# Tokenizer in products of two tokens with overlapped groups, and score products of 32 rows in two attention stages

## The reference, cut to what matters

```python
def _forward(signal):                       # (64, 4000)
    interp = cubic_interpolate_1d(signal, 0.25)
    windows = interp[:, idx]                # (64, 249, 64)
    kw = 0.5 * (windows + 1.3) ** 2 + 0.5 * exp(-0.5 * (windows - 0.7) ** 2)
    M = abs(fft(kw, axis=-1))
    Mmax = max(M, axis=-1, keepdims=True)
    Mt = M * sigmoid(M - 0.12 * Mmax)
    return soft_minimum(Mt, 0.9 * Mmax)     # -log(exp(-a) + exp(-b))
...
q, k, v = heads(x @ Wq.T + bq), heads(x @ Wk.T + bk), heads(x @ Wv.T + bv)   # 4 heads of 16
attn = softmax(einsum('bhnd,bhmd->bhnm', q, k) * 16 ** -0.5)
```

## Time and profile before

| what | us |
|---|---|
| median of 3 runs (lowest, highest) | 5498.31 (5491.29, 5501.21) |
| the profiled execution, its own time | 5488.11 |
| its span, first to last instruction | 5486.3 |
| TensorE busy | 4628.9 (84%) |
| VectorE busy | 2953.6 (54%) |
| ScalarE busy | 2398.0 (44%) |
| mean granted clock of TensorE | 0.858 |

### The profile page before, as it was taken

How to read it: one execution, slowest core, us unless ns; L and a number is a source line. 1 busy time by engine, 2 the same in 40 slices (tenths; PEclk the granted TensorE clock), 3 DMA queues, 4 the chain that set the end, 5 groups by cost and what they waited for, 6 DMA issues and landing times. The chain is left out here.

```text
span 5486.3 us, 115823 instructions
## 1 busy us (share of the span) xinstructions
PE 4628.9 (84%) x33352; PEld 3139.7 (57%) x33352; DVE 2953.6 (54%) x8221; ACT 2398.0 (44%) x6049; POOL 2090.7 (38%) x2436
## 2 busy tenths in 40 slices
PE   4509999566779999889997657699999999979999
PEld 4405666334656666556665644366666666646665
DVE  1144555255535565444443446577777777735554
ACT  3323343242112333334442223277777777735555
POOL 0002222275623343222224756354444444433333
PEclk9998777667957797799996556699999999989999
DMA  0010010132210010043331112100000000033332
GB/s 9 8 34 21 20 22 19 27 99 66 56 26 21 23 27 23 23 93 82 74 79 37 42 42 53 41 8 12 9 12 9 12 9 12 8 67 73 72 73 62
DMA packets 483609, 206.37 MB, mean 38 GB/s; under 512 B 451744, under 2 KB 474454, under 8 KB 483286
## 3 DMA queue, kind: packets, MB, share of 16 engines
q1 hardware_dynamic: 483414, 204.24, 16.5%
HBM read 158.26 MB, written 45.91 MB: 37 GB/s over the span
## 5 line engine op out<-in xcount | busy, mean ns | idle before, releaser
L3346 POOL TENSOR_TENSOR att_P<-att_P,att_rden 125x498 f32<-125x498 f32 x512 | 520.3, 1016 | 640.0 <-DVE att_rden L3617 640.0
L3533 ACT ACTIVATE att_P<-att_pS,att_nb 125x249 f32<-125x249 f32 x1024 | 472.8, 476 | 17.0 <-DVE att_nb L3625 17.0
L2638 DVE TENSOR_TENSOR moe_hT<-moe_silu,moe_pH 128x498 f32<-128x498 f32 x384 | 258.9, 674 | 324.8 <-ACT moe_silu L2624 324.8
L3954 ACT ACTIVATE sw_hT<-sw_pH,sw_b 128x498 f32<-128x498 f32 x512 | 318.3, 673 | 243.4 <-PE sw_pH L3908 243.4
L3449 PEld LDWEIGHTS att_pP<-att_ident,att_P 124*125 124x125 f32 (+1 forms) x2048 | 262.1, 187 | 187.5 <-issue 187.5
L3449 PE MATMUL att_pP<-att_ident,att_P 124*125 124x124 f32 (+1 forms) x2048 | 351.6, 294 | 9.8 <-POOL att_P L3346 8.4
L2624 ACT ACTIVATE moe_silu<-moe_pH 128x498 f32<-128x498 f32 x384 | 225.3, 587 | 284.5 <-PE moe_pH L2581 198.7
L3625 DVE TENSOR_REDUCE att_nb<-att_pS 125x2 f32<-125x498 f32 x512 | 322.6, 667 | 47.1 <-PE att_pS L3437 45.4
L3540 ACT ACTIVATE att_PTr<-att_pP 125x498 f32<-125x498 f32 x512 | 304.7, 595 | 91.6 <-PE att_pP L3449 85.7
L578 POOL TENSOR_TENSOR att_norm_centered<-att_F,att_norm_sum 125x256 f32<-125x256 f32 (+1 forms) x128 | 85.1, 665 | 645.8 <-DVE att_norm_sum L573 645.5
L1013 PE MATMUL att_pS<-att_kT,att_qT 16*125 16x249 f32 x1024 | 302.3, 478 | 2.1 <-ACT att_kT L1119 1.3
(11 more groups left out here) (460 smaller groups left out, 11403.4 us busy)
## 6 DMA issues: line engine op xcount, KB each, us to landing
moe_share<-mixing SPq DMA_DIRECT2D x64, 498.0 KB
sw_share<-mixing SPq DMA_DIRECT2D x64, 498.0 KB
ffn_W<-in_ffn_pairs SPq DMA_DIRECT2D x64, 192.0 KB
att_F<-h_stream SPq DMA_DIRECT2D x192, 62.5 KB
att_X<-h_stream SPq DMA_DIRECT2D x192, 62.5 KB
h_stream<-att_H SPq DMA_DIRECT2D x64, 62.5 KB
ffn_F<-h_stream SPq DMA_DIRECT2D x64, 62.5 KB
ret_F<-h_stream SPq DMA_DIRECT2D x64, 62.5 KB
```

The source lines that it names most:

```text
L3346: g.tensor_tensor(own, own, bc(rden[:, j % 2, c, :], T), ALU.mult).then_inc(*scaled.one())
L3533: ins = a.activation(P[:, r, c, t, :], pS[:, 2 * r + c, t * T:(t + 1) * T], ACT.Exp, bias=nb[:, r, c, t:t + 1], accum_out=den[:, r, c, t:t ...
L3954: a.activation(hT[:, k % 4, :, :], pH[:, place, :, 0:T], ACT.Relu, bias=b1[:, k:k + 1]).then_inc(*hid_ready.one())
```

## The change

The tokenizer is written anew. The host lays the samples out turned (`x_turned`: samples by signals), so nothing is transposed on the chip. Two neighbouring tokens share a product: 36 samples (20 plus a step of 16) are the rows, 128 columns of taps give both tokens' 64 points. 25 groups of `PG` = 5 such products (ten tokens) are written out without a loop. SP loads four groups ahead (`AHEAD`). Each engine's order is by slots: in slot s TensorE interpolates group s and makes the spectrum of group s-1, and the other engines follow the same order, with two buffers of everything. The spectrum is made in halves: each token's 64 points lie in one half of the partitions and give 64 rows of the output there. The passes behind the loop are cut into three chunks of groups (0 to 11, 11 to 22, 22 to 25); a chunk's steps are put into the slots 1 to 6 after its last group, and its store on SP into slot 9 or behind the loop. The sigmoid is one activation.

In attention 0 and attention 1 the score products read 32 rows (`ROOM`) in place of 16 and 17; positions, columns and order are the same.

```diff
-    WG = 8
-    GROUPS = T // WG
-    TAPS = 20
+    PG = 5
+    Q = (T + 1) // 2
+    GROUPS = Q // PG
+    TAPS = 36
     NF = 33
+    COLS = PG * BATCH
+    CHUNKS = ((0, 11), (11, 22), (22, GROUPS))
+    AHEAD = 4
...
+        def chunk_at(s, step):
+            return [c for c, (lo, hi) in enumerate(CHUNKS) if hi + step == s]
...
             def _(sp):
...
+                def load(s):
+                    if s >= AHEAD:
+                        sp.wait_ge(*interpolated.after(s - AHEAD))
+                    k = s % AHEAD
+                    src = A["x_turned"][s * 32 * PG:s * 32 * PG + TAPS, :]
+                    sp.dma_start(xs[:, k, :, :], bass.AP(src.tensor, src.offset, [[BATCH, TAPS], [32 * BATCH, PG],
+                                                                                 [1, BATCH]])).then_inc(
+                        *loaded[k].one())
+                    sp.dma_start(wt[:, k, :, :], A["const_taps"][:, s * PG:(s + 1) * PG, :]).then_inc(
+                        *loaded[k].one())
...
+                load(0)
...
+                for s in range(1, GROUPS):
+                    load(s)
+                    for c in chunk_at(s, 9):
+                        store(c)
+                for c in range(len(CHUNKS)):
+                    if CHUNKS[c][1] + 9 >= GROUPS:
+                        store(c)
...
             def _(pe):
...
+                for s in range(GROUPS + 1):
+                    if s < GROUPS:
+                        u, k = s % 2, s % AHEAD
+                        pe.wait_ge(*loaded[k].after(s // AHEAD))
+                        pe.wait_ge(*squared.after(s - 2))
+                        for q in range(PG):
+                            ins = pe.matmul(pI[:, u, q * BATCH:(q + 1) * BATCH], wt[:, k, q, :], xs[:, k, q, :],
+                                            start=True, stop=True)
+                        ins.then_inc(*interpolated.one())
...
+                        g, u = s - 1, (s - 1) % 2
+                        pe.wait_ge(*windows_ready.after(g))
+                        pe.wait_ge(*squares_ready.after(g - 2))
+                        for q in range(PG):
+                            for w2 in range(2):
+                                r = slice(w2 * 64, (w2 + 1) * 64)
+                                ins = pe.matmul(pM[r, u, q * 2 * NF:(q + 1) * 2 * NF],
+                                                kw[r, u, q * BATCH:(q + 1) * BATCH], dft[r, :], start=True, stop=True)
+                        ins.then_inc(*spectrum.one())
...
             def _(a):
...
+                    for c in chunk_at(s, 1):
+                        q = pairs(c)
+                        a.wait_ge(*power_ready.after(CHUNKS[c][1] - 1))
+                        a.activation(mag[:, q, :], mag[:, q, :], ACT.Sqrt).then_inc(*magnitude_ready.one())
+                    for c in chunk_at(s, 3):
+                        q = pairs(c)
+                        a.wait_ge(*excess_ready.after(c))
+                        a.activation(d[:, q, :], d[:, q, :], ACT.Sigmoid).then_inc(*masked.one())
+                    for c in chunk_at(s, 5):
...
@@ attention 0, by query and by key @@
-                        ins = pe.matmul(pS[:, 2 + s % 2, t * T:t * T + T], qT[r:r + D, u, b, t * OFF:t * OFF + PT],
-                                        kT[r:r + D, u, b, :], start=True, stop=True, tile_position=(r, 0))
+                        ins = pe.matmul(pS[:, 2 + s % 2, t * T:t * T + T], qT[r:r + ROOM, u, b, t * OFF:t * OFF + PT],
+                                        kT[r:r + ROOM, u, b, :], start=True, stop=True, tile_position=(r, 0))
...
-                        ins = pe.matmul(pS[:, s % 2, t * T:t * T + T], kT[r:r + DV, u, b, t * OFF:t * OFF + PT],
-                                        qmT[r:r + DV, b, :], start=True, stop=True, tile_position=(r, 0))
+                        ins = pe.matmul(pS[:, s % 2, t * T:t * T + T], kT[r:r + ROOM, u, b, t * OFF:t * OFF + PT],
+                                        qmT[r:r + ROOM, b, :], start=True, stop=True, tile_position=(r, 0))
@@ attention 1, by query and by key @@
-                    return pe.matmul(pS[:, 2 + s % 2, out], qT[r:r + D, u % 2, b, q], kT[r:r + D, u, b, k],
+                    return pe.matmul(pS[:, 2 + s % 2, out], qT[r:r + ROOM, u % 2, b, q], kT[r:r + ROOM, u, b, k],
...
-                    return pe.matmul(pS[:, s % 2, out], kT[r:r + DV, u, b, k], qmT[r:r + DV, b, q],
+                    return pe.matmul(pS[:, s % 2, out], kT[r:r + ROOM, u, b, k], qmT[r:r + ROOM, b, q],
```

More of the change, by code:

```diff
@@ L387, in stage_tokenizer @@
[L387 to L403, removed]
+        names = "interpolated squared kernels_done windows_ready spectrum squares_ready power_ready"
@@ new lines, in store @@
+                def store(c):
+                    q = pairs(c)
+                    sp.wait_ge(*out_ready.after(c))
+                    for w2 in range(2):
+                        n = min(q.stop, Q - w2) - q.start
+                        dst = h[:, 2 * q.start + w2:2 * q.start + w2 + 1, :]
+                        sp.dma_start(bass.AP(dst.tensor, dst.offset, [[T * C, BATCH], [2 * C, n], [1, C]]),
+                                     out[w2 * BATCH:(w2 + 1) * BATCH, q.start:q.start + n, :]).then_inc(
+                            *stored[c].one())
@@ new lines, in _ @@
+                load(0)
+                for half in range(2):
+                    sp.dma_start(dft[half * 64:(half + 1) * 64, :], A["const_dft"][:, :]).then_inc(*const_loaded.one())
+                for s in range(1, GROUPS):
[5 more added lines that the diff above has]
+                        store(c)
+                for c in range(len(CHUNKS)):
+                    sp.wait_ge(*stored[c].after(0))
@@ L428, in _ @@
             @block.tensor
             def _(pe):
[L430 to L453, removed]
@@ L458, in _ @@
                 a.wait_ge(*memset_done.after(0))
[L460 to L481, removed]
@@ L512, in _ @@
-                groups(v, body)
-                v.wait_ge(*magnitude_ready.after(0))
-                link(v.reduce_max(top[:, :], mag[:, :, :], AX.X))
-                v.tensor_scalar(thr[:, 0, :], top[:, :], 0.12, None, ALU.mult)
-                link(v.tensor_scalar(thr[:, 1, :], top[:, :], 0.9, None, ALU.mult))
-                v.tensor_tensor(d[:, :, :], mag[:, :, :], bc(thr[:, 0, :], NF), ALU.subtract).then_inc(
-                    *excess_ready.one())
-                v.wait_ge(*excess_exp.after(0))
@@ L520, in _ @@
-                link(v.tensor_scalar(d[:, :, :], d[:, :, :], 1.0, None, ALU.add))
-                link(v.reciprocal(d[:, :, :], d[:, :, :]))
-                link(v.tensor_tensor(mag[:, :, :], mag[:, :, :], d[:, :, :], ALU.mult))
-                v.tensor_tensor(lg[:, :, :], mag[:, :, :], bc(thr[:, 1, :], NF), ALU.subtract).then_inc(
-                    *gap_ready.one())
-                link(v.tensor_tensor(mag[:, :, :], mag[:, :, :], bc(thr[:, 1, :], NF), ALU.min))
-                v.wait_ge(*gap_log.after(0))
@@ L4111, in interpolation_taps @@
         w[p // 64, idx - (16 * (p // 64) - 2), p % 64] += val
-    return w
+    both = np.zeros((36, (T + 1) // 2, 2, 64), f)
+    for k in range(2):
+        n = (T + 1 - k) // 2
+        both[16 * k:16 * k + 20, 0:n, k, :] = w[k::2].transpose(1, 0, 2)
+    return both.reshape(36, (T + 1) // 2, 128)
 def constants():
```

179 lines of the change are left out of this document (105 added, 74 removed).

## The result

The changed kernel takes 5081.4 us (median of 4 runs, 5079.0 to 5084.7), the kernel before beside it 5494.8 (5467.1 to 5501.2): a ratio of 0.926, with a 95% interval from 0.922 to 0.929. The profiled execution took 5083.5 us against 5488.1, so 404.6 us went.

What follows compares the result with a forecast made beforehand. The tokenizer was taken as a chain across engines, attention 0 and 1 as bound by TensorE at a falling clock. Gains 241 + 110 + 60 = 411 us bring 5488.1 to 5077, forecast 5087 as median, range 5030 to 5190.

Steps and rivals of the forecast that it cites:

- Tokenizer: gain 241: Tokenizer rewritten with overlapping groups and chunked tail: from 404.5 to 163 us, gain 241, with both ends 225 to 262.
- the bounds' low end of 3.7: TensorE's time for one tokenizer group of ten tokens: 3.7 to 4.8 us, taken as 4.2.
- the case with its halves side by side: Tokenizer's twenty spectrum records a group: 1.3 us if both array halves work side by side, 2.4 one after the other.
- 8 + 3: Tokenizer loop: 8 us for chunk 0's ScalarE activations beyond free time, 3 us for loads waiting behind its store.
- nearly throughout: Sign of being right: TensorE in the tokenizer busy nearly throughout, at about 4.2 us a group.
- 18 by share and 25: Tokenizer's last two stores: 18 us as 56% of the old one, 25 if half was fixed cost; 22 taken.
- Attention 0: 110 forecast: Score products of 32 rows keep attention 0's clock up, pairs about 14.1 us: gain 110 us, between 75 and 120.
- Attention 1: 60 forecast: Wider score products in attention 1, a low stretch staying in most pairs: gain 60 us, between 30 and 95.
- The 20 us for the first pairs: Attention 1's first two or three pairs, low before, could give 20 us more at the upper clock.
- Rival (1): Rows don't count for the clock, only a busy engine; both attentions stay, only the tokenizer gains: 5257 us, chance 0.12.
- Rival (2): The lower clock level keeps itself up in attention 1, which then gives nothing: 5147 us, chance 0.15.
- Rival (3): A wider score product costs time in both attentions; the kernel ends slower, between 5760 and 6260 us, chance 0.02.

Runs made afterwards that it cites:

- the products put into the two thin places: Changed kernel plus seven mask products a pair in attention 1, four ahead of the value products, three ahead of the turn of the heads' output: 5032.7 us.
- the four with fill and increments: Changed kernel with added mask products and VectorE increments: all edits 5017.5 us; increments split 5010.7; split, two chunks 5050.5; two chunks, 105 increments in tokenizer loop 5003.8.
- the increments: Changed kernel with 190 semaphore increments added to VectorE's program behind the tokenizer's last copy: 5057.5 us.

## Why the prediction was right

5087 us were forecast for the median, 5081.4 came, in the range. The sum was 411 us, the profiled execution lost 404.6. That is closer than its terms were, and so in part luck: against the forecast the tokenizer gave 8 us more, attention 0 gave 20 more, attention 1 gave 13 less, and attention 3 and the untouched stages beside it took 16 and 5, which were not in the sum. The 10 us that the forecast adds for the median didn't come either (profiled 5083.5, median 5081.4).

- **Tokenizer: gain 241, measured 249.** Up to the last group, 123 forecast and 121.3 measured, by errors that cancel. A group takes 3.62 us, below the bounds' low end of 3.7: the ten interpolation records took 2.39 as costed from the old spectrum, so the products kept the lower level's price, as counted, and the spectrum cost what the case with its halves side by side gave, 20 records in 1.36 (1.3 forecast). I took 4.2, midway; 25 groups are 15 us less. The chunks in the loop cost 22.7 (with one chunk the last power sum ends at 98.6) where I had 8 + 3. TensorE's waits split it: 10.0 while chunk 0 passes through the loop (five waits for VectorE's sum between 59 and 83 us), near the 8 from ScalarE's free 2.1 us a slot; 7.0 for the loads behind chunk 0's store, where I had 3 and at most 6; and some 5 at the loop's end, where chunk 1's first steps stand on ScalarE and VectorE ahead of the last group's. That last part I had at nothing: the step that failed is the one that counted chunk 0 alone, and beside it the price of the loads. The tail was 34.4 against 40: 16.8 to chunk 1's output (18), and 17.6 for the stores, where I took 22 between 18 by share and 25. That the share fits is luck, since the whole store became shorter too: with one chunk it takes 26.1 us (145.73 to 171.80) where it took 32.8, for the same bytes, and no run shows why. TensorE was busy all through a group, but 91 of 153 us of the stage: "nearly throughout" was wrong.
- **Table loads.** One is 1.28 us, and the activation starts 0.02 us after its end (122.82 + 1.28, 124.12). The drain that the Trainium skill (ScalarE: Activation LUTs, What ACT_TABLE_LOAD costs) puts on top isn't there, and the tail isn't 10 us longer.
- **Attention 0: 110 forecast, 130 measured, above its own range.** The mechanism was right (though the stretch that I gave for the clock's fall, 560 to 566, lies behind it: the score products have the lower level's 0.62 us from 551.81 on). The size of a pair was not: 13.68 us and not 14.1, since what a pair loses at the lower level isn't in proportion to the time it spends there (3.0 us for 6.3 in the pair of 16.70, 7.8 for 18.1 in that of 21.50). And none of TensorE's waits came back: it was busy 382.4 of 383.0 us.
- **Attention 1: 60 forecast, 47 measured.** The low stretch stayed in most pairs, as said, and the products put into the two thin places took it away. Pairs went from 21.63 to 20.45 us. The 20 us for the first pairs didn't come: they stayed at 30.5 and 27.5, the clock rising only 126 us into the stage, as before.
- **Attention 3: not in the sum, 16 us lost.** I followed every engine's program inside the touched stages and nothing of it outside. This is the one mechanism that I missed.

Rival (1) falls by the runs with 18 and 24 rows. Its rule in the Trainium skill (TensorE: Matmul & The Clock Gate, Why this matters for your kernels) is half of what the runs show: a gap did bring the clock down (the wait of 1.79 us), and products put into gaps raised it in attention 1; but TensorE busy 21.40 of 21.40 us stood at 0.58 while it multiplied 16 and 17 rows. Rival (2) was half true, for the first pairs. Rival (3) falls: a step of eight score records takes 1.04 us at the upper level with 32 rows as with 17.

## What to carry to other kernels

In this kernel a product of few rows was no cheaper in time and cost the clock; where padding is there to be read, try reading it, and a harmless product in a gap can pay for itself. When an untouched stage changes, look for idle time that nothing ended, and test it by moving that engine's program by some instructions. And cost work that is put beside a loop by the slots of the engine that does it in order, for every chunk that still meets the loop.

## What the runs showed of the hardware

- **Where a loop stands in an engine's program has a price.** Over the kernel before, the changed one and the twelve experiments, attention 3 took 1313 to 1315 us or 1326 to 1330 and nothing between, and which of the two followed VectorE's program: twenty instructions fewer or 190 more ahead of the loop took away the pause of 1.35 us a pass, and ten fewer brought one of 3.9 into attention 1. The Trainium skill (Runtime: NRT & Kernel Launch, Instruction fetch mechanics) says that instructions come in blocks and that a branch out of the blocks at hand waits for a fetch. The runs agree that position alone decides; a fetch itself no run here shows.
- **A clock that goes up and down comes with scatter.** The kernel before ran between 5443 and 5506 us in these studies, with a mean granted clock of 0.868 in the shortest execution and 0.854 in the longest. The changed kernel stayed within 6 us, and the four with fill and increments that ran four times within 0.6 to 6.4. That the clock is the cause is likely, but no run separates it.
- **What stays open:** why the first pairs of attention 1 start at the upper level in some kernels (19.0 and 17.9 us) and at the lower in others (30.5 and 27.5) with the same products, and with it the 18 us that the increments took off that stage. No run was made for that alone.
